# The first block of each unit's probabilities turned in 32 x 32 squares by VectorE and sorted by transfers, in a two-layer cross-attention kernel

## Chip, cores and metric

The kernel runs on one core of a Trainium2 chip. The metric is the time of one execution on the device in microseconds, the median of several runs.

## The reference

One layer of plain attention and one block with two cross-attention layers and an MLP, over a batch of 8 with 100 queries and 361 context rows each, width 512:

```python
q, k, v = x @ w_q.T, ctx @ w_k.T, ctx @ w_v.T              # single head, width 512
x = x + alpha * (softmax(q @ k.T / sqrt(512)) @ v) @ w_o.T
for i in (1, 2):                                           # 16 heads of 128, same context both times
    h = layer_norm(x)
    kh = concat([ctx @ wk + bk, bias_k]); vh = concat([ctx @ wv + bv, bias_v])
    x = x + softmax((h @ wq + bq) @ kh.T / sqrt(128)) @ vh @ wo + bo
x = x + gelu(layer_norm(x) @ w_fc1 + b_fc1) @ w_fc2 + b_fc2
```

## The kernel before

All products are made in fp32r with each operand split into a high and a low part, three matmuls for one product (`mm3`). The batch is worked on in two halves of four elements (`NB` = 4); with two layers that makes four phases (`PHASES`). Keys and values are never formed. A head's query is sent through the key weights (pieces `k`), so that scores are taken against the raw context columns, and the attended context rows are sent through the value and output weights afterwards (pieces `v` and `o`). The bias key is the first of `T` = 362 columns of scores.

In a phase the 16 x 100 query rows of one batch element are cut into 13 blocks of 125 rows (the last one 100), and these into six units: units 0 to 4 of two blocks, unit 5 of three. A step is a unit k and a batch element b; 24 steps make a phase. In a step TensorE makes the scores of each block x (12 matmuls into one bank), turns its probabilities (three transposes with the identity into one PSUM bank, `turn_probs`, line 1019), and one step later multiplies them with the context rows (`attend`, 36 matmuls). Between these, VectorE takes the maxima (`maxima`, lines 1815 and 1817), ScalarE the exponentials (`exps`, line 1372), VectorE scales them by the reciprocal of the sum (`normalise`, line 1826). From the turned block in PSUM, ScalarE copies the high part (`probs_hi`, line 1147), VectorE takes the low part (`probs_lo`, line 1525) and copies the first row, the weights of the bias key, to `p0_row` (line 1839). ScalarE sends that row to memory (`send_first_row`, line 1387), and SyncE later loads it back on all partitions for the value pieces (`load_first_probs`, line 472).

The order is written out by hand: each engine runs its own program over `STEPS`, with the pieces of weight products placed by `PIECES` at "a" (ahead of the second scores), "m" or "b" (behind attend) of a step. An instruction that waits holds up all that is behind it on its engine. In units 2 and 4 (`LATE`) the first two steps take their scores in another order. SyncE's queue loads the weights, ScalarE's sends the first rows; GpSimd splits the weights (lines 555 and 610). Unit 5 of each phase also makes the layer norm of the other half beside its own work: `hidden_mean` in step (5,1), `hidden_variance` (line 942) and `hidden_roots` (square roots on ScalarE, with two table loads, line 1273) in (5,2), `hidden_scale` on VectorE (line 1729) in (5,2) and (5,3). In step (5,3) ScalarE copies the high parts of the context that was loaded for the next phase; the last phase has no such copies. Line 314 and lines 695 to 697 are helpers, for all waits and for the three matmuls of a product.

## Time and profile before

| what | value |
|---|---|
| median of 3 runs | 1784.81 us (1784.6 to 1786.17) |
| profiled execution | 1782.94 us |
| its span, first to last instruction | 1781.1 us |
| granted TensorE clock | 0.999 of full |
| TensorE busy | 1761.6 us (99%) |
| VectorE, GpSimd, ScalarE busy | 1155.0, 843.9, 745.3 us |
| busy share of the DMA engines | 30.1% (main queue) |

An engine's busy time says how much of the span it worked, not whether the end depended on it; the chain that ended last says that. Times in a timeline are microseconds from the start of the span.

### The profile page before, as it was taken

How to read it: one execution, taken by the hardware profiler on the slowest of the kernel's cores; microseconds unless marked ns; L12 is line 12 of the kernel's file. 1: busy time of each engine (PE TensorE's matmuls, PEld its weight loads, DVE VectorE, ACT ScalarE, POOL GpSimd, SP SyncE). 2: the span in 40 equal slices, each digit the busy share in tenths (PEclk: the TensorE clock that was granted, in tenths of full speed). 3: DMA queues.
4: the chain of work that ended last, by engine and by line, in shares of the span. 5: the costliest groups of instructions: out<-in, count | busy, mean ns of one | idle time of the engine just before them, and what ended most of it. 6: DMA issues, size and time to landing. Idle time of an engine off the chain costs nothing.

```text
span 1781.1 us, 30253 instructions
## 1 busy us (share of the span) xinstructions
PE 1761.6 (99%) x11146; PEld 1715.6 (96%) x11146; DVE 1155.0 (65%) x2705; ACT 745.3 (42%) x1624; POOL 843.9 (47%) x701
## 2 busy tenths in 40 slices
PE   8999999999999999999999999999999999999999
PEld 5899999999999999999999999999999999999999
DVE  3667676666876665657766566668766665676665
ACT  3634333333553333335443333345533333344554
POOL 2774342353584352534863423535834434315554
PEclk9999999999999999999999999999999999999999
DMA  9933231122551211223522211134412122104342
GB/s 261 246 119 86 68 94 40 35 81 81 137 143 35 56 54 52 79 62 99 142 78 52 80 40 56 54 107 123 135 36 62 44 58 80 58 22 142 112 137 78
DMA packets 116165, 156.90 MB, mean 88 GB/s; under 512 B 48344, under 2 KB 63960, under 8 KB 116020
## 3 DMA queue, kind: packets, MB, share of 16 engines
q1 hardware_dynamic: 113300, 150.68, 30.1%
q10 hardware_dynamic: 2720, 4.30, 0.8%
q8 instruction: 90, 1.47, 0.3%
q14 instruction: 55, 0.45, 0.1%
HBM read 149.81 MB, written 5.14 MB: 87 GB/s over the span
## 4 chain that ended last, share of the span: by engine, by line
PE 91%; DVE 4%; DMA 1%; POOL 1%; ACT 1%; issue 1%; SPq 0%; ACTq 0%; DVEq 0%; POOLq 0%
PE psum L695 28%; PE psum L697 28%; PE psum L696 28%; PE psum L1019 4%; PE psum L729 2%; DMA key_stage<-head_w_dram 1%; DVE prob L1826 1%; DVE centred L1729 0%; DVE a_lo L1525 0%; ACT prob L1372 0%; DVE stats L1817 0%; PE psum L708 0%; PE psum L866 0%; PE psum L704 0%; POOL x_held L651 0%
## 5 line engine op out<-in xcount | busy, mean ns | idle before, releaser
L555 POOL TENSOR_TENSOR wbuf_hi<-stage,zero_col 128x512 fp32r<-128x512 f32 x256 | 271.8, 1062 | 694.2 <-PE psum L697 497.0
L610 POOL TENSOR_TENSOR wbuf_lo<-stage,wbuf_hi 128x512 fp32r<-128x512 f32 x256 | 334.9, 1308 | 20.1
L695 PE MATMUL psum<-pT_hi,ctx_rows_hi 121*128 121x250 f32 (+3 forms) x1152 | 332.6, 289 | 0.0
L697 PE MATMUL psum<-pT_hi,ctx_rows_lo 121*128 121x250 f32 (+3 forms) x1152 | 331.3, 288 | 0.0
L696 PE MATMUL psum<-pT_lo,ctx_rows_hi 121*128 121x250 f32 (+3 forms) x1152 | 330.8, 287 | 0.0
L695 PE MATMUL psum<-ctxT_hi,a_hi 128*125 128x362 f32 (+1 forms) x832 | 280.8, 337 | 0.4
L697 PE MATMUL psum<-ctxT_hi,a_lo 128*125 128x362 f32 (+1 forms) x832 | 272.7, 328 | 0.0
L696 PE MATMUL psum<-ctxT_lo,a_hi 128*125 128x362 f32 (+1 forms) x832 | 272.5, 328 | 0.0
L1525 DVE TENSOR_TENSOR a_lo<-psum,a_hi 128x500 fp32r<-128x500 f32 (+2 forms) x288 | 144.2, 523 | 174.1 <-ACT a_hi L1147 174.0
L695 PE MATMUL psum<-a_hi,wbuf_hi 128*128 128x400 f32 x720 | 255.2, 354 | 1.6 <-DVE xT L1744 1.6
L697 PE MATMUL psum<-a_hi,wbuf_lo 128*128 128x400 f32 x720 | 247.6, 344 | 0.0
L696 PE MATMUL psum<-a_lo,wbuf_hi 128*128 128x400 f32 x720 | 247.5, 344 | 0.0
L696 PEld LDWEIGHTS psum<-pT_lo,ctx_rows_hi 121*128 121x128 f32 (+1 forms) x1152 | 219.4, 190 | 0.6
L695 PEld LDWEIGHTS psum<-pT_hi,ctx_rows_hi 121*128 121x128 f32 (+1 forms) x1152 | 218.1, 189 | 0.6
L697 PEld LDWEIGHTS psum<-pT_hi,ctx_rows_lo 121*128 121x128 f32 (+1 forms) x1152 | 218.0, 189 | 0.0
L1147 ACT ACTIVATE a_hi<-psum 128x500 fp32r<-128x500 f32 (+2 forms) x288 | 126.7, 468 | 210.4 <-PE psum L697 210.0
L1372 ACT ACTIVATE prob<-psum,stats 125x362 f32<-125x362 f32 (+1 forms) x208 | 117.3, 564 | 204.8 <-DVE stats L1817 204.7
L1147 ACT ACTIVATE pT_hi<-psum 121x375 fp32r<-121x375 f32 (+1 forms) x208 | 99.9, 480 | 190.5 <-PE psum L1019 190.4
L695 PEld LDWEIGHTS psum<-ctxT_hi,a_hi 128*125 128x125 f32 (+1 forms) x832 | 153.2, 184 | 1.9 <-issue 1.3
L696 PEld LDWEIGHTS psum<-ctxT_lo,a_hi 128*125 128x125 f32 (+1 forms) x832 | 153.4, 184 | 0.7
L697 PEld LDWEIGHTS psum<-ctxT_hi,a_lo 128*125 128x125 f32 (+1 forms) x832 | 153.2, 184 | 0.0
L1744 DVE TENSOR_TENSOR xT<-psum,xT 128x400 f32<-128x400 f32 x296 | 147.8, 562 | 0.0
(197 smaller groups left out, 3450.0 us busy)
## 6 DMA issues: line engine op xcount, KB each, us to landing
stage<-head_w_dram SPq DMA_DIRECT2D x256, 256.0 KB, 2.8
mlp_stage<-mlp_w_dram SPq DMA_DIRECT2D x32, 512.0 KB, 3.6
ctx_rows_in<-ctx_dram SPq DMA_DIRECT2D x20, 726.0 KB
ctxT_in<-ctxT_dram SPq DMA_DIRECT2D x20, 724.0 KB, 6.9
p_b<-p_scratch SPq DMA_DIRECT2D x64, 200.0 KB, 3.6
key_stage<-head_w_dram SPq DMA_DIRECT2D x22, 256.0 KB, 8.5
l0w<-l_w_dram ACTq DMA_DIRECT2D x16, 256.0 KB, 9.1
x_held<-x_scratch SPq DMA_DIRECT2D x4, 800.0 KB, 5.7
```

Source lines behind the costliest of these rows:

```text
L555: return nc.gpsimd.tensor_tensor(out, in_, zero_col[0:in_.shape[0], :].broadcast_to(tuple(in_.shape)), ALU.add)
L610: nc.gpsimd.tensor_tensor(lo, held, hi.bitcast(F32), ALU.subtract).then_inc(stage_free, 1)
L695: pe.matmul(out, a_h, x_hi, start=start, stop=False)
L696: pe.matmul(out, a_h, x_lo, start=False, stop=False)
L697: return pe.matmul(out, a_l, x_hi, start=False, stop=stop)
L729: mm = pe.matmul(bank[j * DC + g], chunk(l0w[2 * j][:, c, :], g), l0w[2 * j + 1][:, c, :], start=(c == 0), stop=(c == DC - 1))
L1019: mm = pe.transpose(bank[PT_BANK][0:t_rows, t * PT_STEP:t * PT_STEP + rows], prob[0:rows, i % 2, t0:t0 + t_rows], ident[0:rows, 0:rows])
L1147: return nc.scalar.activation(out, in_, ACT.Copy)
L1372: nc.scalar.activation(prob[0:rows, i % 2, :], bank[S_BANK + i % 2][0:rows, 0:T], ACT.Exp, bias=st[:, 0:1], accum_out=st[:, 2:3]).then_inc ...
L1525: return nc.vector.tensor_tensor(out, value, hi.bitcast(F32), sub)
L1744: return nc.vector.tensor_tensor(out, value, x, ALU.add)
L1826: nc.vector.tensor_scalar(prob[0:rows, i % 2, :], prob[0:rows, i % 2, :], st[:, 3:4], None, ALU.mult)\
```

## The change

The first block (x = 0) of every step is no longer turned by TensorE. ScalarE writes its exponentials in the order of the columns, VectorE scales them as before and then turns the tile in place in squares of 32 x 32. Four transfers on ScalarE's queue (`sort_squares`), one for each group of 32 partitions, bring the squares to their places in a new tile `sorted0`; `probs_hi` and `probs_lo` read that tile in place of PSUM. For the other blocks ScalarE writes the exponentials in a sorted order of columns, and TensorE turns them as before. The context rows are laid out on the host in the order that this gives, on all 128 partitions in three chunks, where there were 121, 121 and 120 rows. Scores are padded to `W` = 384 columns, masked with a large negative number. To make room, the buffers for broadcast first rows go from four to three and those for single rows from three to two, and one load of first rows moves behind two loads of weights.

```diff
-CH = 121
-CHUNKS = [(0, CH), (CH, CH), (2 * CH, T - 2 * CH)]
+TC = -(-T // P)
+SQUARE = 32
+GROUPS = P // SQUARE
+RUN = TC * SQUARE
+W = GROUPS * RUN
+MASKED = -1e30
-P0_BUFS = 4
-ROW_BUFS = 3
+P0_BUFS = 3
+ROW_BUFS = 2
+def in_squares(k, b, x):
+    return x == 0
...
+        prob = sb("prob", [P, 2, W])
+        sorted0 = sb("sorted0", [P, GROUPS, RUN])
...
+        def sorted_columns(ap):
+            return ap.rearrange("p (t i g) -> p g t i", g=GROUPS, i=SQUARE)
+        def in_order(ap):
+            return ap.rearrange("p (g t i) -> p g t i", g=GROUPS, i=SQUARE)
...
# SyncE, first rows
-                sp.wait_ge(p0_out[s % ROW_BUFS], p0_written(s))
+                for j in range(max(s - ROW_BUFS + 1, 0), s + 1):
+                    sp.wait_ge(p0_out[j % ROW_BUFS], p0_written(j))
...
-                for h in range(H - 4, H):
+                for h in range(H - 4, H - 1):
                     load_first_probs(ph, h)
                 load_weights(ph, W_AT["o", H - 3])
                 load_weights(ph, W_AT["o", H - 2])
+                load_first_probs(ph, H - 1)
                 load_weights(ph, W_AT["o", H - 1])
...
# TensorE
                 def turn_probs(k, b, x):
+                    if in_squares(k, b, x):
+                        return
...
-                        for t, (_, rows) in enumerate(CHUNKS):
-                            mm = mm3(out, chunk(r_hi[0:rows, 3 * b + t, :], m), chunk(r_lo[0:rows, 3 * b + t, :], m),
-                                     pT_hi[0:rows, t, 0:wide], pT_lo[0:rows, t, 0:wide], start=(t == 0), stop=(t == 2))
+                        for t in range(TC):
+                            mm = mm3(out, chunk(r_hi[:, TC * b + t, :], m), chunk(r_lo[:, TC * b + t, :], m),
+                                     pT_hi[:, t, 0:wide], pT_lo[:, t, 0:wide], start=(t == 0), stop=(t == TC - 1))
...
# ScalarE
-                    nc.scalar.activation(prob[0:rows, i % 2, :], bank[S_BANK + i % 2][0:rows, 0:T], ACT.Exp,
+                    out = (in_order if in_squares(k, b, x) else sorted_columns)(prob[0:rows, i % 2, :])
+                    nc.scalar.activation(out, in_order(bank[S_BANK + i % 2][0:rows, 0:W]), ACT.Exp,
                                          bias=st[:, 0:1], accum_out=st[:, 2:3]).then_inc(s_exp, 1)
+                def sort_squares(k, b, x):
+                    at = k, b, x
+                    if not in_squares(*at):
+                        return
+                    n = sorted_blocks(ph, at)
+                    act.wait_ge(squares_turned, ph * Q_LAYER + Q_AT[at] + 1)
+                    if n > 0:
+                        used_in, user = divmod(n - 1, len(BY_HELD[x]))
+                        act.wait_ge(pt_lo, used_in * S_LAYER + T_AT[BY_HELD[x][user]] + 1)
+                        act.wait_ge(p0_kept, used_in * S_LAYER + T_AT[BY_HELD[x][user]] + 1)
+                    for a in range(GROUPS):
+                        squares = prob[a * SQUARE:(a + 1) * SQUARE, S_AT[at] % 2, :].rearrange("i (g f) -> i g f", g=GROUPS)
+                        act.dma_start(held[x][:, a, :], squares).then_inc(sorted_ld[x], 16)
...
+                    if in_squares(k, b, x):
+                        act.wait_ge(sorted_ld[x], GROUPS * 16 * (sorted_blocks(ph, (k, b, x)) + 1))
+                        copy(in_columns(pT_hi[:, :, square_columns(k, x)]), held_chunks(x)).then_inc(pt_hi, 1)
...
                         run_pieces((k, b, "a"))
+                        sort_squares(k, b, 0)
                         if (k, b) == VARIANCE_IN:
                             hidden_roots(ph)
...
# VectorE
+                    if g < 2:
+                        nc.vector.memset(bank[4 + g][0:L, T:W], MASKED).then_inc(masked_s, 1)
+                    nc.vector.memset(bank[4 + g % 2][0:L, 0:1], MASKED).then_inc(masked_s, 1)
...
+                    if in_squares(k, b, x):
+                        dve.wait_ge(s_norm, ph * S_LAYER + i + 1)
+                        nc.vector.transpose(prob[:, i % 2, :], prob[:, i % 2, :]).then_inc(squares_turned, 1)
...
+                    if in_squares(k, b, x):
+                        turned, to = held_chunks(x), square_columns(k, x)
+                        low(in_columns(pT_lo[:, :, to]), turned, in_columns(pT_hi[:, :, to])).then_inc(pt_lo, 1)
...
+                if ph == 0:
+                    nc.vector.memset(prob[:, :, :], 0.0).then_inc(prob_set, 1)
+                    dve.wait_ge(prob_set, 1)
```

## Rows read from the trace of the kernel before

**Rows 1.** The page's first line of busy times, and the chain by line

```profile
PE 1761.6 (99%) x11146; PEld 1715.6 (96%) x11146; DVE 1155.0 (65%) x2705; ACT 745.3 (42%) x1624; POOL 843.9 (47%) x701
by line: PE psum L695 28.4%; PE psum L697 28.0%; PE psum L696 28.0%; PE psum L1019 3.6%; PE psum L729 1.6%; DMA key_stage<-head_w_dram 0.8%; issue 0.7%; DVE prob L1826 0.7%; DVE centred L1729 0.4%; DVE a_lo L1525 0.4%; ACT prob L1372 0.3%; 
```

**Rows 2.** TensorE's waits: who for whom, us in total, times, longest

```profile
PE psum L695 <- DVE xT L1744: 1.8, 3, 1.4
PE psum L942 <- POOL x_held L651: 1.8, 4, 0.4
```

**Rows 3.** Timeline of TensorE around one turn: start, duration (a pipeline's, so overlapping)

```profile
707.49 0.27 PE L696 MATMUL psum<-pT_lo,ctx_rows_hi 120*128 120x250 f32 x1
707.60 0.28 PE L697 MATMUL psum<-pT_hi,ctx_rows_lo 120*128 120x250 f32 x1
...
708.23 0.35 PE L696 MATMUL psum<-h_lo,wbuf_hi 128*128 128x400 f32 x1
708.41 0.34 PE L697 MATMUL psum<-h_hi,wbuf_lo 128*128 128x400 f32 x1
```

**Rows 4.** Groups of TensorE by form: busy us, mean ns, idle before

```profile
L696 PE MATMUL psum<-pT_lo,ctx_rows_hi 121*128 121x250 f32 x640 | 179.2, 280 | 0.0
...
L696 PE MATMUL psum<-pT_lo,ctx_rows_hi 120*128 120x250 f32 x320 | 88.7, 277 | 0.0
...
L1019 PE MATMUL psum<-ident,prob 125*121 125x125 f32 x384 | 74.0, 273 | 1.6 <-DVE p_row L1839 1.6
```

**Rows 5.** VectorE's split of a turned block (busy, mean) and its scaling (min/median/max ns)

```profile
L1525 DVE TENSOR_TENSOR pT_lo<-psum,pT_hi 121x375 fp32r<-121x375 f32 x192 | 104.3, 543 | 10.0 <-ACT pT_hi L1147 2.5
...
L1826 DVE TENSOR_SCALAR prob<-prob,stats x208: 407/409/1316, 144.1 to 1602.0; 125x362 f32<-125x362 f32 x96, 100x362 f32<-100x362 f32 x8
```

**Rows 6.** Issues of transfers by line, min/median/max ns; the landing is of L472

```profile
L1387 ACTq DMA_DIRECT2D p_scratch<-p_row x208: 221/221/485, 149.3 to 1604.9; - x104
...
L472 SPq DMA_DIRECT2D p_b<-p_scratch x64: 359/377/1041, 183.2 to 1606.7; - x64
...
DMA to landing us min/median/max: 3.0/3.6/5.0
...
L493 SPq DMA_DIRECT2D s_cols<-s_scratch x4: 619/660/896, 133.2 to 1266.9; - x4
```

**Rows 7.** Timeline of a plain step in unit 1, several engines

```profile
552.92 0.41 DVE L1826 TENSOR_SCALAR prob<-prob,stats 125x362 f32<-125x362 f32 x1
...
558.25 0.48 ACT L1147 ACTIVATE pT_hi<-psum 121x375 fp32r<-121x375 f32 x1
...
560.45 0.49 ACT L1147 ACTIVATE pT_hi<-psum 121x375 fp32r<-121x375 f32 x1 [1.71 <-PE psum L1019]
...
560.97 0.55 DVE L1525 TENSOR_TENSOR pT_lo<-psum,pT_hi 121x375 fp32r<-121x375 f32 x1 [0.16 <-ACT pT_hi L1147]
...
562.23 0.28 PE L695 MATMUL psum<-pT_hi,ctx_rows_hi 121*128 121x250 f32 x1
```

**Rows 8.** Timeline of steps (5,2) and (5,3) in phase 1, several engines

```profile
826.04 1.28 ACT L1273 ACT_TABLE_LOAD   x1 [0.36 <-DVE p_row L1839]
...
829.44 0.55 ACT L1372 ACTIVATE prob<-psum,stats 125x362 f32<-125x362 f32 x1
...
838.39 0.54 PE L1019 MATMUL psum<-ident,prob 100*121 100x100 f32 x3
...
840.58 1.09 DVE L1826 TENSOR_SCALAR prob<-prob,stats 125x362 f32<-125x362 f32 x1
...
840.77 1.49 ACT L1147 ACTIVATE ctx_rows_hi<-ctx_rows_in 121x1536 fp32r<-121x1536 f32 x1 [0.42 <-DVE p_row L1839]
...
844.88 0.56 ACT L1372 ACTIVATE prob<-psum,stats 125x362 f32<-125x362 f32 x1 [1.32 <-DVE stats L1817]
...
852.27 0.54 PE L1019 MATMUL psum<-ident,prob 100*121 100x100 f32 x3
```

**Rows 9.** Timeline of VectorE in step (5,3) of the last phase

```profile
1597.13 0.59 DVE L1525 TENSOR_TENSOR a_lo<-psum,a_hi 128x250 fp32r<-128x250 f32 x2 [0.89 <-ACT a_hi L1147]
```

More of the change, by code:

```diff
@@ L113 @@
 S_LAYER = len(S_AT)
+def in_squares(k, b, x):
+    return x == 0
+HELD = 1
+BY_PE = [at for at in TURNED if not in_squares(*at)]
+PE_AT = {at: i for i, at in enumerate(BY_PE)}
+PE_LAYER = len(BY_PE)
+IN_SQUARES = [at for at in TURNED if in_squares(*at)]
+Q_AT = {at: i for i, at in enumerate(IN_SQUARES)}
+Q_LAYER = len(IN_SQUARES)
+BY_HELD = [[at for at in IN_SQUARES if at[2] == j] for j in range(HELD)]
 PARTS = [2 if len(unit) == 2 else DC for unit in UNITS]
@@ L303, in build @@
         p0_ld = [sem(f"p0_ld{j}") for j in range(P0_BUFS)]
+        masked_s, prob_set, squares_turned = sems("masked_s prob_set squares_turned")
+        sorted_ld = [sem(f"sorted_ld{j}") for j in range(HELD)]
         y_mm, y_hi, y_done = sems("y_mm y_hi y_done")
@@ L564, in ctx_rows_lo @@
                 pool.wait_ge(cr_hi_s, use * NB + b + 1)
-                per = 3 if use < TURNS else 1
-                for t in range(3 * b, 3 * b + 3, per):
+                per = TC if use < TURNS else 1
+                for t in range(TC * b, TC * b + TC, per):
                     at = slice(t, t + per)
-                    done = nc.gpsimd.tensor_tensor(r_lo[0:CH, at, :], r_in[0:CH, at, :], r_hi[0:CH, at, :].bitcast(F32),
+                    done = nc.gpsimd.tensor_tensor(r_lo[:, at, :], r_in[:, at, :], r_hi[:, at, :].bitcast(F32),
                                                    ALU.subtract)
@@ L780, in turn_probs0 @@
                     wait(pe, lp_lo, g)
-                    for t, (t0, rows) in enumerate(CHUNKS):
-                        mm = pe.transpose(bank[6][0:rows, t * L:(t + 1) * L], prob0[0:L, g % 2, t0:t0 + rows], ident[0:L, 0:L])
+                    for t in range(TC):
+                        mm = pe.transpose(bank[6][:, t * L:(t + 1) * L], chunk(prob0[0:L, g % 2, :], t), ident[0:L, 0:L])
                     mm.then_inc(lp_mm, 1)
@@ L791, in attend0 @@
                     wait(pe, lu_copied, g)
-                    for t, (_, rows) in enumerate(CHUNKS):
-                        mm = mm3(bank[7][0:L, :], p0_hi[0:rows, g % 2, t, :], p0_lo[0:rows, g % 2, t, :],
-                                 r_hi[0:rows, 3 * b + t, :], r_lo[0:rows, 3 * b + t, :], start=(t == 0), stop=(t == 2))
+                    for t in range(TC):
+                        mm = mm3(bank[7][0:L, :], p0_hi[:, g % 2, t, :], p0_lo[:, g % 2, t, :],
+                                 r_hi[:, TC * b + t, :], r_lo[:, TC * b + t, :], start=(t == 0), stop=(t == TC - 1))
                     mm.then_inc(lu_mm, 1)
@@ L1012, in turn_probs @@
                     pe.wait_ge(s_norm, ph * S_LAYER + i + 1)
-                    turn = ph * S_LAYER + T_AT[k, b, x]
-                    if T_AT[k, b, x] == 0:
+                    turn = PE_AT[k, b, x]
+                    if turn == 0:
                         pe.wait_ge(s0_row, ph + 1)
-                    wait(pe, pt_lo, turn)
-                    wait(pe, p0_kept, turn)
-                    for t, (t0, t_rows) in enumerate(CHUNKS):
-                        mm = pe.transpose(bank[PT_BANK][0:t_rows, t * PT_STEP:t * PT_STEP + rows],
-                                          prob[0:rows, i % 2, t0:t0 + t_rows], ident[0:rows, 0:rows])
+                    else:
+                        pe.wait_ge(pt_lo, ph * S_LAYER + T_AT[BY_PE[turn - 1]] + 1)
+                        pe.wait_ge(p0_kept, ph * S_LAYER + T_AT[BY_PE[turn - 1]] + 1)
+                    for t in range(TC):
+                        mm = pe.transpose(bank[PT_BANK][:, t * PT_STEP:t * PT_STEP + rows],
+                                          chunk(prob[0:rows, i % 2, :], t), ident[0:rows, 0:rows])
                     mm.then_inc(pt_mm, 1)
@@ L1415, in layer @@
                         send_first_row(k, b, 0)
+                        sort_squares(k, b + 1, 0)
                         exps(k, b, 1)
@@ L1814, in maxima @@
                     scored = bank[S_BANK + i % 2][0:rows, 0:T]
+                    if ph == 0 and i < 2:
+                        nc.vector.memset(bank[S_BANK + i][0:rows, T:W], MASKED).then_inc(masked_s, 1)
                     nc.vector.tensor_copy(scored[:, 0:1], s0_cols[0:rows, j, b:b + 1]).then_inc(s_col, 1)
@@ L2016 @@
         "ctxT": rows(np.moveaxis(context[:, :T], 1, 2)),
-        "ctx": context,
+        "ctx": context.reshape(B, GROUPS, TC, SQUARE, D).transpose(0, 3, 1, 2, 4).reshape(B, P, TC, D),
         "l0_w": np.stack([rows(a["L0_xattn_w_q"]), rows(a["L0_xattn_w_k"]), rows(a["L0_xattn_w_v"]),
```

82 lines of the change are left out of this document (51 added, 31 removed).

## The prediction

> **What bounds the kernel now.** I read the busy shares and the chain that ended last first. TensorE is busy 99% of the span, and its matmuls make up nearly all of the chain; the other engines hide behind it [rows 1]. In the list of what TensorE waited for the entries are of a few microseconds in total; the two that the change touches have 1.8 us each [rows 2]. So a TensorE instruction that goes away is worth its whole time, as long as the other engines still deliver. The turns of probabilities (line 1019) are 3.6% of the chain, 64 us for 208 blocks, or 0.31 us each [rows 1]. A stretch of instructions gives the price directly: the matmul ahead of a turn starts at 707.60, the second one behind it at 708.23. Of these 0.63 us, 0.11 and 0.18 us are what the neighbours take anyway (from the starts before and after), so the turn costs 0.34 us [rows 3]. The 273 ns of one transpose [rows 4] is its latency in a pipeline, not its price: three of them would make 0.8. I take 0.33 us a block.
>
> **What the change removes.** Block x=0 of each of 24 steps in four phases, 96 blocks: 96 x 0.33 = 31.7 us of TensorE. The attended matmuls now contract over 128 rows and not 121 and 120, with the same columns. From 120 to 121 rows the mean goes from 277 to 280 ns [rows 4], which is at the limit of ends that are modelled: cost 0. If 3 ns a matmul were real, 3456 of them would cost 10 us; that goes into the upper end. The turns that stay move as many columns: 0.
>
> **What it adds on VectorE.** One square transpose per first block, 384 elements in SBUF. No row shows one. The nearest is the split of a turned block, 375 elements at 0.54 us; below lies the scaling of the same tile at its usual 0.41 us, above that scaling at its slowest, 1.32 us [rows 5]. I take 0.57, in total 55 us on an engine that is 65% busy. The masks (memsets in the first score maxima) and the one clearing of `prob` meet little cover at the start: an estimate of 0.5 us, since the chain there goes through VectorE; bounds 0 and 2. The exponentials of 384 for 362 columns stay hidden.
>
> **What it adds on ScalarE's queue.** Four transfers per first block, each of 128 pieces of 384 B. ScalarE waits for VectorE's transpose before it issues them, and all that is behind them in program order waits too. ScalarE's transfer of one piece costs 0.22 us to issue, SyncE's of 512 pieces of 400 B 0.38, the scattered one of line 493 0.66 [rows 6]. The 512-piece one is nearest in form: 0.38, so 1.5 us a block; bounds 0.9 and 2.6.
>
> **A plain step**, one without pieces [rows 7]. The scaling of block 0 ends at 553.33, its transpose at 554.0; the last of four issues starts at 555.1 and ends at 555.5. The exponentials of block 1 slip behind them by a microsecond, and their block is turned only 5 us later: free. `probs_hi` of block 0 ran at 558.25. If the squares land later than that, the path from there is: that copy, its split, the first row and its send, then copy and split of the last block, which ended at 561.52. That is 3.3 us, of which about 0.5 are ScalarE's wait for TensorE ahead of 560.45: 2.8. Attend began at 562.23, now at 561.9. So the squares may land at 559.1, 4.0 us after the last issue began. The transfer of 512 small pieces took 3.0 to 5.0 us, median 3.6 [rows 6], and here the last transfer carries only a quarter of them: cost 0. Where a piece stands ahead of the sort, a product (12 matmuls of 0.18, 2.2 us) moves attend by more than it moves the issue: about 5.7 us. Units 2 and 4 have more.
>
> **The last unit.** Here the change costs time, and phase 1 shows where [rows 8]. In step (5,2) `sort_squares` stands ahead of `hidden_roots`. ScalarE began to load the root table at 826.04; now it waits for the transpose (827.0) and issues until 828.5. What is behind slips 2.4 us, first the exponentials of block 1 (829.44). VectorE sat waiting for them and then has work nearly without a gap up to the scaling of block 2, for which TensorE waits ahead of 838.39: 0.2 us are absorbed, 2.2 stay. In step (5,3) the scaling of block 0 ended at 841.67, now 843.9; transpose to 844.6, issues to 846.1; only then come the two context copies that began at 840.77 and take 2.9 us, and the exponentials of block 1: 849.0 for 844.88, 4.1 us. VectorE goes on without a gap to the scaling of block 2, which TensorE awaits ahead of 852.27. One more term: `probs_lo` of block 0 now has two SBUF operands while GpSimd works on the context. The scaling, in SBUF too, takes 1.09 us there [rows 8] and 0.41 elsewhere [rows 5]; I add 0.6. So 4.8 us at the unit's end in the three phases that reload the context. The last phase has no such copies, and VectorE has gaps of 0.89 us behind its block 1 [rows 9]: there 2.2 us stay.
>
> The Trainium skill ("SBUF — State Buffer", "SBUF: two separate sides") says that a GpSimd instruction and a VectorE one with two SBUF inputs or in a two-port mode shut each other out of a shared port, each for a whole instruction. The slow scalings agree with it. By that rule the transpose and the new split could each lose up to a GpSimd instruction in (5,3), twice what the row alone makes me charge, and the time would be some 4 us longer; that is on the way to rival B and in its chance.
>
> The slips swallow the gains of this unit's later turns: TensorE waits in `hidden_variance` for GpSimd's sums in every phase, 0.4 us [rows 2], and these hang on the end of attend, not on the turn. So only the 20 steps before and (5,0) pay: 21 x 4 x 0.33 = 27.7 us.
>
> **The rest.** Three waits for VectorE's additions, 1.8 us in all [rows 2], get longer with a longer VectorE program: +1.0 (bounds 0 and 3). With three buffers for broadcast rows the load of head 15 moves behind weights o14; five products, 11 us, lie between attend's end and its use, against a landing of 3.6: 0. With two row buffers the copy of a first row waits for the send two blocks back, which is a step old: 0. If either cover is gone, it is one 3.6 us load a phase.
>
> **Sum.** -27.7 + 3 x 4.8 + 2.2 + 1.0 + 0.5 = -9.6 us. The profiled execution took 1782.9 us (span 1781.1), so 1773.3; the median of the runs is 1.9 us above it: 1775.
>
> **Rivals.**
> A. The slips are small: issues 0.22 us, transpose 0.41, no conflict. Then (5,2) slips 1.5 and (5,3) 2.5: -27.7 + 3 x 2.5 + 1.5 + 1 = -18, 1767. With no slip at all and the start free, -32, 1753. For it: an issue can be that cheap. Against: only one with a single piece is.
> B. All is given back in the last unit: issues 0.66 us, transpose 1.3. (5,2) slips about 4.1, (5,3) 7.7: -27.7 + 3 x 7.7 + 4.1 + 3 = +2.5, 1787. For it: VectorE is full there and passes each slip on. Against: that issue price is of one scattered form.
> C. Slower, by landings. The 12 plain steps ((0,3), (1,0), (3,0) in four phases) are at their limit at 4.0 us; each microsecond more costs 12 us, and from 5.7 us on 52 further steps pay. It decides at 12 x late = 9.6 + 3.6, a landing of 5.1 us. At 6.5 us: 12 x 2.5 + 52 x 0.8 - 10 = about +60, 1845. For it: the slowest of the 512-piece transfers took 5.0 us. Against: their median.
> The Trainium skill ("DMA: Bandwidth & Descriptors", "Specifications") says that transfers below 512 B miss line rate; these pieces are of 384 B, which speaks for C. No row here shows the size of a piece by itself.
>
> **Chances.** Forecast 0.48 (own range 1771 to 1781), A 0.20, B 0.15, C 0.17. About 0.2% (3.6 us) is what a measurement tells from no change. Faster by more: A and nearly all of the forecast, 0.67; same, B: 0.15; slower, C and a rest of B: 0.18. The range goes from half-way between A and its bound to just past B, 1758 to 1790, takes in attended matmuls that are 3 ns longer, and leaves out C.
>
> **What would show it.** 112 blocks turned by TensorE at the same 0.33 us; VectorE's transposes near 0.57 us; ScalarE's issues near 0.38; each phase some 7 us shorter up to its last unit; in that unit new waits of TensorE for the scaling, some 2 us each, ahead of the turns of (5,2,2) and (5,3,2); no wait at attend in plain steps. The prediction is wrong if landings pass 5 us, if attended matmuls grow with 128 rows, or if issues take as little as 0.22 us.

## The result, and the profile after

The changed kernel takes 1844.0 us (median of four runs, 1840.9 to 1845.6) against 1784.7 us for the kernel before on the same chip (1784.6 to 1786.2). The ratio is 1.0332, with a 95% interval of 1.0319 to 1.0345: 59 us slower, where 10 us faster was forecast. The profiled execution took 1842.7 us, with a span of 1840.9.

The page of the changed kernel: busy shares, the granted TensorE clock by slices, the chain, and the groups of the exponentials and the attended matmuls.

```profile
PE 1753.8 (95%) x10858; PEld 1695.1 (92%) x10858; DVE 1233.8 (67%) x2813; ACT 769.3 (42%) x1624; POOL 850.1 (46%) x701
...
PEclk9999999999899999998999999999999999999999
...
PE 71%; DVE 14%; ACT 5%; ACTq 4%; issue 3%; DMA 3%; POOL 0%; DVEq 0%; SPq 0%; POOLq 0%
...
L1428 ACT ACTIVATE prob<-psum,stats 125x384 f32<-125x384 f32 (+1 forms) x208 | 161.4, 776 | 307.0 <-DVE stats L1897 174.6
...
L741 PE MATMUL psum<-pT,ctx_rows_hi 128*128 128x250 f32 (+1 forms) x1152 | 334.3, 290 | 4.8 <-DVE pT L1601 4.5
```

Where nearly the whole chain was TensorE's [rows 1], a quarter now belongs to VectorE, ScalarE, its queue and transfers. The list of what TensorE waited for (total us, times, longest) says for whom; before the change the turn (there line 1019) waited 2.4 us in all for the scaling, and no entry was above the 4.6 of the load of `l0w`. First the one line of before, then the list after:

```profile
PE psum L1019 <- DVE prob L1826: 2.4, 4, 0.7
```
```profile
PE psum L1068 <- DVE prob L1906: 37.1, 20, 4.6
PE psum L741 <- issue: 7.5, 8, 1.1
PE psum L741 <- DVE a_lo L1605: 6.7, 4, 2.2
PE psum L775 <- DMA l0w<-l_w_dram: 5.8, 1, 5.8
PE psum L741 <- DVE a_lo L1601: 5.7, 4, 1.4
PE psum L741 <- DVE xT L1822: 4.7, 9, 2.0
PE psum L741 <- DVE pT L1601: 4.5, 6, 1.8
PE psum L741 <- DVE a_lo L1610: 4.5, 4, 1.3
```

L1068 is the turn, L1906 the scaling in front of it, the `a_lo` lines splits of attended values and of values, the line with `pT` the split of a sorted block. The groups on the tile of probabilities, with count and minimum/median/maximum in ns (first and last start follow):

```profile
L1443 ACTq DMA_DIRECT2D sorted<-prob x384: 550/624/1752, 148.1 to 1653.0; - x192
L1428 ACT ACTIVATE prob<-psum,stats x208: 572/932/968, 146.1 to 1660.6; 125x384 f32<-125x384 f32 x96, 100x384 f32<-100x384 f32 x8
L1910 DVE STREAM_TRANSPOSE prob<-prob x96: 578/578/580, 147.5 to 1650.5; 128x384 f32<-128x384 f32 x96
```

An issue takes 0.62 us, four of them 2.5. An exponential of a first block takes 0.58 us, one of another block, whose output goes to every fourth element, 0.93.

**Where the time went.** In each kernel's trace I took the starts of the 96 attended products and subtracted, stretch by stretch, the lengths of before. In 51 of the 95 stretches TensorE is 0.24 to 0.42 us faster, 17.3 us in all: the removed turns are there. The four stretches that begin with the attend of (4,3), (5,0), (5,1) and (5,2) hold the steps (5,0) to (5,3), since a step is attended one step later; they are 20.4, 6.6, 22.7 and 7.3 us longer (sums over four phases), 56.9 in all. Those that begin at (1,3) and (3,3) are 9.8 longer, the first three of the phases 5.4; the start is 2.5 later; the other stretches together are 15.0 shorter. The sum is +59.6 us, the difference of the spans 59.8.

The first of them, in phase 1, is 5.1 us longer and begins in step (5,0). The timeline (start, duration; in brackets idle time and what ended it) of ScalarE, then VectorE, then TensorE:

```profile
813.61 2.66 ACTq L1443 DMA_DIRECT2D sorted<-prob  x4
816.38 0.94 ACT L1428 ACTIVATE prob<-psum,stats 125x384 f32<-125x384 f32 x1 [4.13 <-issue]
817.17 1.06 ACT L1196 ACTIVATE a_hi<-psum 128x500 fp32r<-128x500 f32 x2
822.25 0.53 ACT L1196 ACTIVATE pT<-sorted 128x384 fp32r<-128x384 f32 x1 [4.01 <-DMA sorted<-prob]
825.08 0.59 ACT L1405 ACTIVATE a_hi<-psum,cols 128x400 fp32r<-128x400 f32 x1 [2.30 <-DVE psum L1865]
...
817.89 1.26 DVE L1601 TENSOR_TENSOR a_lo<-psum,a_hi 128x500 fp32r<-128x500 f32 x2
822.80 0.70 DVE L1601 TENSOR_TENSOR pT<-sorted,pT 128x384 fp32r<-128x384 f32 x1 [3.65 <-ACT pT L1196]
823.43 1.06 DVE L1928 COPY p_row<-sorted 1x128 f32<-1x128 f32 x1
824.42 0.62 DVE L1865 SCALAR_TENSOR_TENSOR psum<-p_b,dv_cols,psum 128x400 f32<-128x400 f32 x1
825.70 0.63 DVE L1605 SCALAR_TENSOR_TENSOR a_lo<-psum,cols,a_hi 128x400 fp32r<-128x400 f32 x1 [0.66 <-ACT a_hi L1405]
...
818.71 0.42 PE L741 MATMUL psum<-a_hi,wbuf_hi 128*128 128x400 f32 x1 [1.44 <-DVE a_lo L1601]
826.39 0.45 PE L741 MATMUL psum<-aside_hi,wbuf_hi 128*128 128x400 f32 x1 [1.44 <-DVE a_lo L1605]
```

There are two mechanisms in these lines. First, while ScalarE issues, nothing behind it in its program moves: the exponentials start at 816.38, the copies of attended values at 817.17, their splits at 817.89, and a product that reads them waits 1.44 us. Second, the squares are there only six us after the last issue ended, where the median landing is 2.1 us from the issue; other loads fill the queues (from 815 to 820 the DMA engines are 82% busy and move 285 GB/s); the copy of `pT`, the copy of its first row (1.06 us for a usual 0.21) and, in program order behind them, the values of a head are late, and TensorE waits 1.44 us again. A third stall of 1.28 us follows at 828.81, a fourth of 0.46 at 834.81. Then the turns of (5,1,2), (5,2,2) and (5,3,2) wait 2.44, 4.57 and 2.59 us, each behind a chain of ScalarE's issues, its exponentials of block 1, and a VectorE that has no gap above 0.4 us from there to the scaling of block 2. In each of the four steps ScalarE stands still for some 4 us (4.13 in the lines above): 2.5 of issues, and before them the wait for the scaling and the transpose. The stalls drag the clock along. Windows of TensorE (busy us and count, granted clock, DMA share, GB/s) around the longest wait, and the matmuls behind it:

```profile
860.00:865.00 5.00, 3.72 (x24) 1.00 0.84 273
865.00:870.00 5.00, 1.71 (x7) 0.59 0.09 33
870.00:875.00 5.00, 5.00 (x24) 0.73 0.15 30
875.00:880.00 5.00, 5.00 (x33) 1.00 0.16 22
```
```profile
868.29 0.76 PE L1068 MATMUL psum<-ident,prob 100*128 100x100 f32 x3 [4.57 <-DVE prob L1906]
...
869.50 0.50 PE L743 MATMUL psum<-ctxT_hi,a_lo 128*125 128x362 f32 x1
869.80 0.50 PE L741 MATMUL psum<-ctxT_hi,a_hi 128*125 128x362 f32 x1
...
872.78 0.32 PE L742 MATMUL psum<-pT,ctx_rows_hi 128*128 128x350 f32 x1
```

From 868.75 to 872.5 twelve matmuls of 362 columns start 0.30 us apart and not 0.17: the lower level of 1.2 GHz, after an idle stretch, and 1.6 us lost on top of the wait. Over the last unit of each phase, from the attend of (4,3) to that of (5,3), the windows are (here and above: the stretch, its length, TensorE busy and its matmuls, granted clock, DMA share, GB/s):

```profile
425.08:499.98 74.90, 61.09 (x354) 0.94 0.41 125
812.92:889.61 76.69, 62.48 (x353) 0.91 0.39 120
1203.64:1279.82 76.18, 62.96 (x354) 0.91 0.39 118
1592.38:1664.76 72.38, 61.86 (x353) 0.93 0.19 54
```

Before the change the clock in the same stretches was 1.00 in all four. TensorE's waits in them add up to 51.7 us against 5.5. Of the 56.9 us, 46.2 are thus waits and the removed turns are some -5.3 (16 by 0.33); the 16 that remain are my estimate of what the lower clock costs here. No run isolates it.

### The profile page after: what moved, and what is told of

Same layout as the page of the kernel before. It is cut to its first block, busy times and chain, and to the rows that moved or that the text cites. A ratio compares the mean times of both kernels' runs of the same rounds, so it can differ in the third digit from the quotient of the medians.

```text
span 1840.9 us, 30173 instructions
## 1 busy us (share of the span) xinstructions
PE 1753.8 (95%) x10858; PEld 1695.1 (92%) x10858; DVE 1233.8 (67%) x2813; ACT 769.3 (42%) x1624; POOL 850.1 (46%) x701
## 3 DMA queue, kind: packets, MB, share of 16 engines
q8 instruction: 88, 1.44, 0.3%
## 4 chain that ended last, share of the span: by engine, by line
PE 71%; DVE 14%; ACT 5%; ACTq 4%; issue 3%; DMA 3%; POOL 0%; DVEq 0%; SPq 0%; POOLq 0%
PE psum L741 23%; PE psum L742 22%; PE psum L743 22%; ACTq L1443 3%; DMA sorted<-prob 2%; ACT prob L1428 2%; DVE prob L1906 2%; DVE pT L1601 2%; PE psum L1068 2%; PE psum L775 2%; DVE a_lo L1601 2%; DVE p_row L1928 1%; DVE prob L1910 1%; ACT pT L1196 1%; DVE stats L1897 1%
## 5 line engine op out<-in xcount | busy, mean ns | idle before, releaser
L741 PE MATMUL psum<-pT,ctx_rows_hi 128*128 128x250 f32 (+1 forms) x1152 | 334.3, 290 | 4.8 <-DVE pT L1601 4.5
L742 PE MATMUL psum<-pT,ctx_rows_hi 128*128 128x250 f32 (+1 forms) x1152 | 330.9, 287 | 0.0
L743 PE MATMUL psum<-pT,ctx_rows_lo 128*128 128x250 f32 (+1 forms) x1152 | 329.9, 286 | 0.0
L1428 ACT ACTIVATE prob<-psum,stats 125x384 f32<-125x384 f32 (+1 forms) x208 | 161.4, 776 | 307.0 <-DVE stats L1897 174.6
L742 PE MATMUL psum<-ctxT_lo,a_hi 128*125 128x362 f32 (+1 forms) x832 | 277.8, 334 | 0.0
L741 PEld LDWEIGHTS psum<-pT,ctx_rows_hi 128*128 128x128 f32 x1152 | 218.4, 190 | 11.9 <-DVE pT L1601 10.1
L742 PEld LDWEIGHTS psum<-pT,ctx_rows_hi 128*128 128x128 f32 x1152 | 218.7, 190 | 0.6
L743 PEld LDWEIGHTS psum<-pT,ctx_rows_lo 128*128 128x128 f32 x1152 | 218.3, 189 | 0.0
L1601 DVE TENSOR_TENSOR a_lo<-psum,a_hi 128x500 fp32r<-128x500 f32 (+2 forms) x288 | 138.4, 518 | 67.9 <-ACT a_hi L1196 67.1
L1904 DVE RECIPROCAL stats<-stats 125x1 f32<-125x1 f32 (+1 forms) x208 | 33.1, 159 | 215.2 <-ACT prob L1428 212.7
L741 PEld LDWEIGHTS psum<-a_hi,wbuf_hi 128*128 128x128 f32 x720 | 136.0, 189 | 27.5 <-issue 17.7
L1196 ACT ACTIVATE a_hi<-psum 128x500 fp32r<-128x500 f32 (+2 forms) x288 | 119.8, 472 | 86.3 <-PE psum L743 86.0
```

The source lines that it names most:

```text
L741: pe.matmul(out, a_h, x_hi, start=start, stop=False)
L742: pe.matmul(out, a_h, x_lo, start=False, stop=False)
L743: return pe.matmul(out, a_l, x_hi, start=False, stop=stop)
L1196: return nc.scalar.activation(out, in_, ACT.Copy)
L1428: nc.scalar.activation(out, in_order(bank[S_BANK + i % 2][0:rows, 0:W]), ACT.Exp, bias=st[:, 0:1], accum_out=st[:, 2:3]).then_inc(s_exp, 1)
L1601: return nc.vector.tensor_tensor(out, value, hi.bitcast(F32), sub)
```

## The experiments

My theory after this reading: the loss is made in the last unit, first by ScalarE's 2.5 us of issues, with late landings, the transpose and the slower exponentials as further parts, all on engines that pass slips on. The rivals: it is the landings (C), VectorE, or the exponentials. In the diffs, minus is the changed kernel, if nothing else is said. The table at the end has every kernel's stretches, each from one profiled execution.

**1. Unit 5 turned by TensorE.**
```diff
 def in_squares(k, b, x):
-    return x == 0
+    return x == 0 and k < 5
```


> The squares are used in units 0 to 4 only; the 16 first blocks of unit 5 are turned by TensorE again (exponentials keep the new, strided order). From attend to attend the two traces differ by +57 us over the four stretches that follow the attend of (4,3), by +0.7 us over all the others together, and by +2.5 us before the first. Theory (the loss is made by the last unit's sorts): about 1788 us, the last unit's waits for the scaling gone. Rival 1 (the strided exponentials, +0.37 us each, are what the last unit pays for): 1800 us or more. Rival 2 (the loss is spread over all steps): 1830.

Measured: 1789.5 us, ratio 1.0030 (1.0019 to 1.0041). The last unit's +56.9 became +4.3: 55 of the 59 us go away when this unit is turned by TensorE again. But the 80 turns still removed gain nothing beside run 2.

**2. The layout alone** (`in_squares` returns False).

> No block goes by squares: TensorE turns all 208, but 384 columns, 128 rows, masks, strided exponentials (0.93 us for 0.56) and the fewer buffers stay. Theory: 1785 to 1788, all of this is hidden except at the start and, if anywhere, in the full last unit. Rival (strided exponentials on the path of the last unit, 12 blocks a phase by 0.37 us): 1800.

Measured: 1789.5 us, ratio 1.0028 (1.0019 to 1.0037). 5.3 us of stretches, all in the last unit. A little above what the theory gave; the exponentials there are not hidden.

**3. Exponentials written flat.**
```diff
-                    out = (in_order if in_squares(k, b, x) else sorted_columns)(prob[0:rows, i % 2, :])
+                    out = in_order(prob[0:rows, i % 2, :])
```


> The exponentials of blocks turned by TensorE are written in the order in which they are read (its output columns are then in another order than the reference's; the work is the same). The ACTIVATE should fall from 0.93 to 0.58 us. Theory (ScalarE's queue is what is late in the last unit, so everything on it counts): two such blocks a step, 0.35 us each, at two or three steps of the unit in four phases: 6 to 12 us less than the change, 1832 to 1838. Rival (exponentials hidden): 1844. Rival (they are the main cause): below 1800.

Measured: 1831.5 us, ratio 1.0258 (1.0241 to 1.0275). 12.6 us less than the change; part of the loss, not its main cause.

**4. The copies do not wait for the landing.** `held_chunks` gives the identity tile, and `probs_hi` waits for the transpose. A sort still waits until the sorts before it have landed, and the exponentials until the squares have left their buffer; in the trace those that are put down to this begin 0.1 us behind the last issue, but for one at 0.4.
```diff
-                        act.wait_ge(sorted_ld[x], GROUPS * 16 * (sorted_blocks(ph, (k, b, x)) + 1))
+                        act.wait_ge(squares_turned, ph * Q_LAYER + Q_AT[k, b, x] + 1)
```


> Copy, split and first row of a sorted block read a fixed tile and do not wait for the transfers to land (the probabilities of first blocks do not reach the output); transposes, issues and all else stay. Theory (late landings count only where other loads fill the queues, in (5,0), and at the start of phase 0): 5 us in each of four phases and 3 at the start, so 1820 to 1828. Rival C of the prediction (the landings are the loss): 1785 or less. Rival (they cost nothing): 1844.

Measured: 1820.5 us, ratio 1.0201 (1.0185 to 1.0218). The size was right, the places half: 11.4 us came from the last unit, but 10.1 from (1,3) and (3,3). There the copy of the sorted block waits for the landing in (2,0) and (4,0), and the values of a head behind it are late. ScalarE, VectorE and TensorE of the changed kernel in step (2,0) of phase 1:

```profile
642.82 0.53 ACT L1196 ACTIVATE pT<-sorted 128x384 fp32r<-128x384 f32 x1 [2.35 <-DMA sorted<-prob]
...
646.66 0.63 DVE L1605 SCALAR_TENSOR_TENSOR a_lo<-psum,cols,a_hi 128x400 fp32r<-128x400 f32 x1 [0.66 <-ACT a_hi L1405]
...
647.40 0.42 PE L741 MATMUL psum<-a_hi,wbuf_hi 128*128 128x400 f32 x1 [1.02 <-issue]
```

That split of values ends 0.1 us before TensorE goes on. Counted from the start of the attend of (1,3), it begins after 11.2 us in the changed kernel, after 10.1 in run 4 and after 10.5 in the kernel before. The last of the three loads of weights there has landed after 9.2 us in the changed kernel and after 9.0 in run 4, so the weights do not make the difference.

**5. One transfer of four.** Only the first group of partitions is sent, and the waits count one landing.
```diff
-                    for a in range(GROUPS):
+                    for a in range(1):
```


> Of the four transfers of a sorted block only the first is made (three quarters of the sorted tile keep old values). ScalarE's queue is held 0.6 us a block for 2.5, and the landing comes that much earlier. Not waiting for the landing alone gave 24 us. Theory (issues on ScalarE and landings in traffic share the last unit's loss): the slips of 1.9 us a step go from three or four turns in each last unit on top, so 1795 to 1808. Rival (landings only): 1820. Rival (VectorE's transpose and its own fullness are the loss): 1830 or more.

Measured: 1776.7 us, ratio 0.9951 (0.9935 to 0.9967), 67 us less than the change and more than the theory's range. The last unit is at +15.3, (1,3) and (3,3) at -2.7, and 70 stretches are shorter by 25.5 us. This run takes away 1.9 us of issues, three quarters of the bytes and an earlier landing at once, so it is an upper bound for the issues.

**6. No square transpose.** A copy of one element in its place; the sorted blocks stay unturned.
```diff
-                        nc.vector.transpose(prob[:, i % 2, :], prob[:, i % 2, :]).then_inc(squares_turned, 1)
+                        nc.vector.tensor_copy(stats[0:1, i % 2, 3:4], stats[0:1, i % 2, 3:4]).then_inc(squares_turned, 1)
```


> The square transpose is replaced by a copy of one element; sort and the rest stay (the sorted blocks are not transposed). Theory: 0.4 us less work in each step of a last unit in which VectorE passes every slip on, and sorts that start 0.4 us earlier: 0.8 us by three or four turns by four phases, 10 to 13 us less: 1831 to 1834. Rival (VectorE is the bound of the last unit): 25 us less or more. Rival (hidden): 1844.

Measured: 1816.2 us, ratio 1.0163 (1.0127 to 1.0199), 28 us less. The four runs spread from 1807.8 to 1821.3, so the 28 has some 7 us of play either way; the profiled execution, whose stretches the table has, was the fastest, 35 less. My figure was less than half of it. In that execution 17.6 us came from the last unit and 7.2 from (1,3) and (3,3).

**7. Only the fewer buffers**, in the kernel before.
```diff
-P0_BUFS = 4
-ROW_BUFS = 3
+P0_BUFS = 3
+ROW_BUFS = 2
```


> The kernel before with three buffers for broadcast rows and two for first rows and no other edit (the load of head 15 keeps its place in the queue ahead of the weights). Theory: 0, 1784.7. Rival: the load of head 15 holds the weights behind it, some microseconds a phase: 1790 or more.

Measured: 1791.6 us, ratio 1.0036 (1.0023 to 1.0050). The theory fell: the last of four loads of broadcast rows waits for a free buffer, and SyncE holds the weights behind it. SyncE's timeline, here and then in the kernel before:

```profile
859.40 9.93 SPq L472 DMA_DIRECT2D p_b<-p_scratch  x4
869.38 24.57 SPq L409 DMA_DIRECT2D stage<-head_w_dram  x10
```
```profile
854.66 3.46 SPq L472 DMA_DIRECT2D p_b<-p_scratch  x4
858.17 27.14 SPq L409 DMA_DIRECT2D stage<-head_w_dram  x10
```

It costs 1.8 us between phases, 5.4 in all, and 1.7 more in the last units. The change moves that load behind two loads of weights, and in its trace and in run 2 this stretch is not longer (53.7 to 54.1 us for 54.0): with the move the buffers cost nothing there, as the prediction said.

**8. Twelve chosen steps.** `in_squares` is true only for (1,0), (1,1), (1,3), (2,1), (2,2), (2,3), (3,0), (3,1), (3,3), (4,1), (4,2) and (4,3).

> Squares only in the twelve steps (1,0), (1,1), (1,3), (2,1), (2,2), (2,3), (3,0), (3,1), (3,3), (4,1), (4,2), (4,3), in whose stretches TensorE gained 0.27 to 0.41 us in every phase. 48 turns by 0.35 = 16.8 us less; against it what the layout alone costs, 5 us. Theory: 1773. Rival (the losses move to other steps): 1784 or more.

Measured: 1782.4 us, ratio 0.9984 (0.9970 to 0.9998). 9 us short. The layout's cost stayed, and the stretches behind (1,1) and (3,1) grew by some 0.46 us in seven of eight cases: in (1,3) the transpose of 0.58 us stands ahead of VectorE's additions to xT, for which the next product waits. Those two steps, (1,3) and (3,3), give back what they gain; run 14 leaves them out, and the growth is gone.

**9. Exponentials that read in the sorted order.** The columns are sorted by the read from PSUM, and SBUF is written in one run.
```diff
-                    out = (in_order if in_squares(k, b, x) else sorted_columns)(prob[0:rows, i % 2, :])
-                    nc.scalar.activation(out, in_order(bank[S_BANK + i % 2][0:rows, 0:W]), ACT.Exp,
+                    out, read = prob[0:rows, i % 2, :], bank[S_BANK + i % 2][0:rows, 0:W]
+                    if not in_squares(k, b, x):
+                        out, read = out.rearrange("p (t i g) -> p t i g", g=GROUPS, i=SQUARE), read.rearrange("p (g t i) -> p t i g", g=GROUPS, i=SQUARE)
+                    nc.scalar.activation(out, read, ACT.Exp,
```


> The exponentials of blocks turned by TensorE read PSUM in the sorted order and write SBUF in one run, where the change reads in runs and writes every fourth element. The output is the same. Theory (what costs 0.35 us is the write of single elements, not the order): 0.58 us an ACTIVATE and the time of the kernel with flat exponentials, 1831. Rival (any strided side costs the same): 0.93 us and 1844.

Measured: 1829.8 us, ratio 1.0254 (1.0239 to 1.0269), as with flat exponentials. The group of this kernel:

```profile
L1430 ACT ACTIVATE prob<-psum,stats x208: 557/581/585, 145.3 to 1648.7; 125x384 f32<-125x384 f32 x96, 100x384 f32<-100x384 f32 x8
```

The strided write cost 0.35 us an exponential, the strided read of PSUM costs nothing. Of the 12.1 us by which the sum of this run's stretches is lower, 7.7 are in the last unit. The Trainium skill ("SBUF — State Buffer", "Door 1: The DMA port swizzle") says that SBUF wants at least two accesses to each line of 16 bytes; every fourth fp32 element is one access a line. The trace agrees: 0.93 us for 0.58. A read would also be slowed in PSUM, whose lines it gives as 8 bytes, but of that it speaks for matmuls; for ScalarE's read these rows show no loss.

**10. All issues by SyncE.** `sort_squares` on SyncE, ahead of the weights whose turn comes then; ScalarE keeps it in units 0 and 1 of phase 0. The main lines, in SyncE's program:
```diff
...
+                    for k, b in sorted_before.get(i, []):
+                        if ph > 0 or k > 1:
+                            sort_squares(ph, k, b)
                     for h in VALUES:
                         if P0_READ_AT[h] == i and UNIT_OF[h] < LAST_UNIT:
                             load_first_probs(ph, h)
                     load_weights(ph, i)
...
                         reload_ctx_columns(ph, b)
+                        sort_squares(ph, LAST_UNIT, b + 1)
                         reload_ctx_rows(ph, b)
```


> The four transfers of a sorted block are issued by SyncE, ahead of the weights whose turn comes then (by ScalarE only in units 0 and 1 of phase 0). The output is the same. Theory (2.5 us of ScalarE's time a block are the largest part of the loss; one transfer for four gave 67 us): 1780 to 1795, ScalarE's stalls for them gone; the landings in the last unit's traffic stay. Rival (SyncE comes to them late, or the weights behind them do): above 1810. Rival (the gain of one transfer for four was the bytes or the earlier landing): above 1820.

Measured: 1845.9 us, ratio 1.0344 (1.0320 to 1.0369). As a forecast the theory missed by 50 us; its mechanism held in the last unit, which fell from +56.9 to +8.1. But (1,3) and (3,3) rose from 9.8 to 44.3, and (1,0) and (3,0) rose too. SyncE's timeline in step (2,0) of phase 1:

```profile
633.89 7.93 SPq L535 DMA_DIRECT2D sorted<-prob  x8
641.93 1.63 SPq L517 DMA_DIRECT2D p_b<-p_scratch  x3
643.61 17.39 SPq L453 DMA_DIRECT2D stage<-head_w_dram  x8
```

Two sorts, each with its waits for VectorE, keep the loads of first rows back to 641.9, 9.0 us after the start of the attend of (1,3); in the changed kernel the first begins 1.0 us before it and the others 1.8 us after it. TensorE waits 3.7 us at 647.6 for what hangs on them.

**11 and 12. The same with exponentials that read strided,** and this with unit 5 turned by TensorE.

> Both edits, issues by SyncE and exponentials that read strided. If the exponentials fall to 0.58 us: some 8 us less than with the issues by SyncE alone. If not: the same.

> Both edits, and unit 5 turned by TensorE. 80 turns by 0.33 are 26 us; the first units of phase 0 and the start give some 7 back. Theory: 1765 to 1770, a version that beats both kernels. Rival (the other engines give it back as they did with ScalarE's issues, 1789): 1780 or more.

Measured: 1839.6 us, ratio 1.0308 (1.0287 to 1.0330), and 1839.5 us, 1.0302 (1.0287 to 1.0317). The first is 6 us better, near what was expected. The second missed by 70 us for the reason of run 10; the last unit, at +0.9 without that edit, had nothing left to gain.

**13. Issues by SyncE in unit 5 alone**, with strided reads. Minus is the kernel of run 11; ScalarE keeps the sorts of units 0 to 4.
```diff
-                if (k, b) <= (LAST_UNIT, 0):
+                if (k, b) == (LAST_UNIT, 0):
                     sorted_before.setdefault(max(pieces_before(k, b) + WBUFS, early + 2), []).append((k, b))
```


> All first blocks by squares and exponentials that read strided; the transfers of unit 5 alone are issued by SyncE, those of units 0 to 4 by ScalarE. In units 0 to 4 nothing of SyncE's other loads is moved, and in unit 5 ScalarE is free of the issues. Stretches of the kernel with strided reads for units 0 to 4, and those of the kernel with all issues on SyncE for the four that follow the attend of (4,3), add up to 1829.8 - 41 = 1789. Theory (ScalarE's issues in the last unit make most of the loss): 1785 to 1792. Rival (the last unit's relief came from delays ahead of it): 1815 or more.

Measured: 1785.8 us, ratio 1.0004 (0.9995 to 1.0013). Beside run 9 it moves 16 sorts to another queue and nothing else, and it takes 44 us away: the last unit goes from +49.2 to +0.7. It takes off ScalarE both the issues and the wait for the transpose ahead of them. An issue costs nearly the same there, 603 ns in the median. All landings were within 4.0 us:

```profile
L535 SPq DMA_DIRECT2D sorted<-prob x64: 542/603/1094, 426.0 to 1596.0; - x64
...
DMA to landing us min/median/max: 2.0/2.0/4.0
```

SyncE's order also puts each sort behind the load of context columns and ahead of that of rows, so the earlier landings are part of the 44 us; run 4 puts the landings' share in this unit near 11. TensorE's clock in the last units is back at 1.00 as well, so the 44 include what it cost.

**14. Ten steps**, (1,3) and (3,3) left out, with strided reads.

> Exponentials read strided; squares in ten steps, (1,0), (1,1), (2,1), (2,2), (2,3), (3,0), (3,1), (4,1), (4,2), (4,3): those of the chosen twelve less (1,3) and (3,3), where the transpose of 0.58 us delayed the additions that TensorE waits for and gave back 0.46 us of 0.41. 40 turns by 0.35 are 14 us, the start takes 1.5. Theory: 1772, a version that beats both. Rival (fewer buffers and masks cost what the layout alone cost): 1776 to 1778.

Measured: 1776.0 us, ratio 0.9946 (0.9932 to 0.9959). Both kernels are beaten, by 4 us less than expected. The time is also the rival's, which had the fewer buffers and masks cost what run 2 had lost; run 15 speaks against that reason. In phases 0 and 3 TensorE waited 2.29 us for the squares of (1,0); ScalarE in phase 3:

```profile
1309.26 2.51 ACTq L1448 DMA_DIRECT2D sorted<-prob  x4
...
1317.72 0.53 ACT L1199 ACTIVATE pT<-sorted 128x384 fp32r<-128x384 f32 x1 [4.13 <-DMA sorted<-prob]
```

The last issue ends at 1311.8, the squares are there at 1317.7: SyncE had issued a load of broadcast rows at 1310.05 and two of weights up to 1311.5. This is rival C's mechanism, at single places.

**15. The layout alone, with strided reads.**

> No block by squares, exponentials read strided. The layout alone with strided writes was 5 us slower. Theory (3.5 of them are the exponentials in the full last unit, the rest the start): 1785 to 1787. Rival (it is the buffers or the wider VectorE operations): 1789 again.

Measured: 1782.4 us, ratio 0.9982 (0.9972 to 0.9992). The 5 us of run 2 were the exponentials; the rest of the layout costs nothing outside the start and may gain a little.

**16. Nine steps**, (1,0) left out as well.
```diff
+SORTED_STEPS = [(1, 1), (2, 1), (2, 2), (2, 3), (3, 0), (3, 1), (4, 1), (4, 2), (4, 3)]
 def in_squares(k, b, x):
-    return x == 0
+    return x == 0 and (k, b) in SORTED_STEPS
```


> As the kernel with ten steps, less (1,0). In two phases its squares landed so late, behind a load of broadcast rows and three of weights, that TensorE waited 2.3 us; in the other two TensorE gained 0.4. Theory: 5.0 us less waiting and 1.3 less of stretched matmuls behind it, against 4 by 0.35 given up: 5 us less than 1776, 1771. Rival (another step's squares land late in its place, or the waits come and go with the execution): 1776.

Measured: 1772.4 us, ratio 0.9925 (0.9912 to 0.9939), the fastest of all. In its page and its list of waits TensorE is as full as before the change:

```profile
PE 1746.3 (99%) x11038; PEld 1695.1 (96%) x11038; DVE 1182.2 (67%) x2753; ACT 747.2 (42%) x1624; POOL 842.8 (48%) x701
```
```profile
PE psum L1071 <- DVE p_row L1935: 2.5, 4, 0.6
PE psum L1071 <- DVE prob L1911: 2.3, 4, 0.7
...
PE psum L744 <- DVE xT L1827: 1.9, 3, 1.4
```

All in one table: differences from the trace of before, in us, summed over the four phases, worked out from the starts of the attended products. The execution of run 3 was 6 us above its median, that of run 4 was 5 above and that of run 6 was 8 below.

| kernel | run | start | (0,0) to (0,2) | (1,3), (3,3) | (4,3) to (5,2) | others |
|---|---|---|---|---|---|---|
| the change | - | +2.5 | +5.4 | +9.8 | +56.9 | -15.0 |
| unit 5 by TensorE | 1 | +2.3 | +2.7 | +10.6 | +4.3 | -13.9 |
| layout alone | 2 | +1.6 | -0.2 | 0.0 | +5.3 | -0.6 |
| exponentials flat | 3 | +2.0 | +3.8 | +9.4 | +52.3 | -13.1 |
| no wait for landing | 4 | +2.4 | +8.0 | -0.3 | +45.5 | -13.4 |
| one transfer of four | 5 | +1.2 | -4.2 | -2.7 | +15.3 | -16.9 |
| no square transpose | 6 | +2.4 | +0.1 | +2.6 | +39.3 | -19.6 |
| fewer buffers | 7 | +2.2 | -0.1 | 0.0 | +1.7 | +5.4 |
| twelve steps | 8 | +3.5 | -0.2 | +1.8 | +6.0 | -13.0 |
| strided reads | 9 | +1.7 | +2.9 | +7.5 | +49.2 | -13.8 |
| issues by SyncE | 10 | +1.7 | +1.5 | +44.3 | +8.1 | +3.9 |
| SyncE and strided reads | 11 | +2.3 | +1.8 | +45.1 | +0.9 | +5.4 |
| the same, unit 5 by TensorE | 12 | +2.6 | -0.3 | +46.3 | -1.2 | +5.5 |
| SyncE in unit 5 | 13 | +2.2 | +2.4 | +9.3 | +0.7 | -14.1 |
| ten steps | 14 | +1.7 | -0.6 | +1.3 | +0.7 | -6.8 |
| layout, strided reads | 15 | +2.1 | -0.6 | +0.2 | -0.8 | -2.4 |
| nine steps | 16 | +2.0 | -0.3 | +0.8 | -0.8 | -13.8 |

## Why the prediction was wrong

**The step that failed** is that of the last unit: "only the 20 steps before and (5,0) pay", with slips of 2.2 and 4.8 us in (5,2) and (5,3) alone. It rested on two things. The term "0.38, so 1.5 us a block" for the issues was mis-sized: each took 0.62 us, 2.5 a block, near the upper bound of 2.6. In the prediction's own walk this one microsecond more makes 3.2 us of the slip in (5,2) and 6.8 of that in (5,3), and the unit dearer by 7 us: 1782, not 1844. The price was taken from a transfer of 512 pieces, when the scattered one of line 493, at 0.66 [rows 6], was the nearer; the number of pieces was not what counted. The larger part is that the walk through the unit began at (5,2). In (5,0) and (5,1) ScalarE's copies of attended values stand behind the sort as well, and TensorE stalled there first. Summed over the phases:

| step | forecast | measured |
|---|---|---|
| (5,0) | -1.3 | +20.4 |
| (5,1) | 0 | +6.6 |
| (5,2) | +8.8 | +22.7 |
| (5,3) | +7.8 | +7.3 |

That (5,0) had no slack stood in the list of waits before the change, in an entry that the prediction passed over: the turn's 2.4 us for the scaling are four waits of 0.5 to 0.7 us in this very step, the one of phase 1 at 810.57. A third thing was in no term: the lower clock behind the stalls, some 16 us by my estimate above. Run 13 shows where the loss comes from: it goes when ScalarE neither waits nor issues for these sorts, apart from the share of the earlier landings. With 0.6 us of issues a block, run 5, the time was 1776.7, near the forecast of 1775; part of that agreement is chance, since its landings were earlier too.

**Removed turns**, 0.33 us each: right. The stretches that lost a turn and gained no wait are 0.24 to 0.42 us shorter. **Attended matmuls** of 128 rows at cost 0: right, 290 ns in the mean for the first of the three forms, where the page of before has 289. **Square transpose** 0.57 us: 0.578. All 96 took 578 to 580 ns, so the slowing beside GpSimd that the prediction allowed for in (5,3) did not touch it. The split of a sorted block was slowed in (5,1) (1.39 us at 845.71, 0.55 in the median), not in (5,3) (0.62 at 880.56); there the copy of its first row took 0.99, for a median of 0.21. And that the engine is 65% busy was no cover: run 6 prices the transpose at 28 us.

**"The exponentials of 384 for 362 columns stay hidden"**: wrong twice. Not the columns but the strided output made 112 of them 0.37 us longer, and in the last unit they are on the path: 13 to 14 us of the change in all (runs 3 and 9), some 7 with no squares at all (runs 2 and 15).

**Plain steps, landing**: right in the main. The median landing was 2.1 us, the limit 4.0, and in (1,0) and (3,0) all eight stretches gained 0.29 to 0.40 us; in (0,3) the gain was lost, 1.7 us in all. Out of sight were the landings beside other loads: 39 of the 384 took more than 4.0 us, up to 7.3 in (5,0) and up to 5.1 in the other steps, nearly all of them in (0,3), (1,0), (2,0), (3,0) and (4,0). Rival C had the number, 1845, and a part of the mechanism: 24 us of the loss go with the copies' wait for the landing, 36 stay (run 4). That the number fits is chance.

**(1,3) and (3,3)**, 9.8 us, were in no term. These stretches hold the steps (2,0) and (4,0). In seven of the eight the values of a head are late behind the copy of the sorted block, which waits for the landing, and the copy of its first row, 1.06 us there; TensorE stalls 0.8 to 1.1 us. Run 4 takes the whole 9.8 away. In the eighth, phase 0, TensorE waits 2.03 us at 257.17 for the low parts of weights. The prediction said that units 2 and 4 have more cover than a plain step, and did not look at what else stands behind the copy.

**Additions to xT** +1.0: measured 4.7 us of waits where 1.8 were, +2.9, at the bound of 3. **Start** +0.5: 2.5, but run 7, which has neither masks nor the clearing of `prob`, shows 2.2. The wait for the first load of `l0w` was 5.8 us against 4.6; what of the rest is the change is open. **Buffers** 0: right between the phases, with the move.

**What stays open** is an exact split. The parts found by taking one away (28 for the transpose, 24 for the landing, 13 for the exponentials, and 44, from run 9, for moving 16 sorts off ScalarE) exceed the 59 us, because each restores slack that the others use up, and because a stall lowers the clock behind it.

## What to carry to other kernels

Price an added wait or issue at the place where its engine has the least slack, and walk through every step there: here 16 of 96 blocks made 57 of 59 us, while elsewhere the same edit gained in some steps what it lost in others. An entry of a few tenths of a microsecond in the list of waits marks such a place. A queue of transfers is an engine's time: where four issues of 0.62 us stand, and the wait ahead of them, decided more here than what they move, and each queue has its own cargo that is late next. And an edit that gains in some steps and loses in others is to be made in the former only: nine steps of 24, with the strided write gone, made the kernel 13 us faster.

## What the runs showed of the hardware

A transfer of 32 partitions by 4 runs of 384 B to 128 partitions takes 0.62 us of ScalarE's queue in the median and 0.60 of SyncE's, where one of a single piece takes 0.21. It landed after 2.1 us in the median, and the last two of a block after 6.3 to 7.3 us in (5,0), where other loads kept the DMA engines 82% busy in phase 1. ScalarE's exponential of 384 elements takes 0.58 us written in one run, read in runs or strided, and 0.93 when it writes every fourth fp32 element. VectorE's copy of 128 elements on one partition from SBUF took 0.21 us in the median and 1.06 at 823.43, where GpSimd was working from 823.17 to 824.42; copies out of PSUM in the same places took 0.27.
